# First unit's score granules among the last projections, two sets of part buffers, weight squares one unit later

## The chip, the cores and the metric

The kernel runs on one core of a Trainium2 chip. The metric is the device time of one execution in microseconds; three executions gave 525.33, 525.71 and 528.45, the median is 525.71. The engines work side by side and meet at semaphores only: TensorE (PE, matmuls, with its weight loads as PEld), VectorE (DVE), ScalarE (ACT), GpSimd (POOL), SyncE (SP, which here only issues transfers). Transfers run on 16 DMA engines.

## The reference

One transformer layer on x of 4 batches x 512 tokens x 256 features, float32:

```python
qkv = x @ w_attn + b_attn                      # 16 heads of 16
q, k = rope(q), rope(k)                        # the angle depends on the head
attn = softmax(causal(q @ k.T)) * 256 ** -0.5
x = layernorm(x + (attn @ v) @ w_proj + b_proj)
top 2 of 8 experts by softmax(x @ router_w.T), weights normalised
y = sum over the chosen e: w[e] * (silu(x @ gate_e.T) * (x @ up_e.T)) @ w2_e.T    # FF = 512
x = layernorm(x + y)
```

## The kernel before, in words

**Projections (lines 268 to 422).** TensorE projects each batch in float32: for the four column blocks c of queries and keys two matmuls of 512 columns into bank c (`L416`), then the values of four token tiles (`L397`) into banks 4 to 6 in turn. The rotation is folded into the weights beforehand. Each query and key block is split into three bfloat16 parts whose sum is the float32 value. ScalarE adds the bias (`QF`, L311) and rounds to the first part (`PB[c][:, 0]`, L315); VectorE subtracts to the rest `R1` (L380); ScalarE rounds the rest to the middle part (L303); VectorE subtracts again to the last part (`last_part`, L374). VectorE also adds the values' bias (`values`, L369). The semaphore `l` counts last parts.

There is one buffer `PB[c]` of parts per block for all batches. SyncE stores it to `qk_dram` after the last part (L532, two transfers a block, 8 a batch), and ScalarE may only round the next batch into it when that store has landed (`s_pb`). Between the batches' stores SyncE issues the seven loads (L520, `load_unit`) of one unit of batch 0. All of these are issued in one order on one queue: stores of batch b, loads of unit (0,b), next b; then `XB`, then the eight 1 MB loads of the expert weights w1 (L526), then the loads of unit (1,0) and so on. The loads of unit (b,g) wait until the transposed scores of unit (b-1,g) are done, since they reuse its buffer `KQ[g]`.

**Units (lines 425 on).** A unit is four heads of one batch: 16 units (b,k), each worked on in a step of ten granules n. Within a step the engines carry three units at once. TensorE computes the scores of unit u (`S`, L1168, 96 rows: six products of parts) granule by granule into banks 0 and 1; VectorE reduces each granule to row maxima (L877) and signals `Sf`, on which granule n + 2 waits. GpSimd splits the maxima (L581), TensorE transposes them, ScalarE writes them as extra rows (L747). For unit u - 2 TensorE forms transposed scores into banks 2 to 5 (`ST`, L1189 and L1190), ScalarE takes exponentials (L724), TensorE multiplies with the values (L1207). The order of everything within a step is written out by hand in tables of (k, n). In steps (0,0) and (0,1) ScalarE has no exponentials yet.

The expert weights are scaled by their mean square. `SQUARES_AT` gives the places (b, k, n) at which ScalarE squares the next 4 KB-per-partition piece of w1, 16 pieces in all (L755); a pair needs one landed w1 load. Their sum is formed on TensorE before step (2,0) (L1346).

TensorE starts the units only when all `qf` and all eight value sums are there. GpSimd does nothing in the projections. After the units, 39 expert tiles of 128 tokens follow, and a last normalisation.

Of the kernel before, what the change touches and what calls it, by code (L numbers as in the profile page):

```python
# [24 lines left out]
BF16 = mybir.dt.bfloat16  # L25
# [3 lines left out]
ALU = mybir.AluOpType  # L29
ACT = mybir.ActivationFunctionType  # L30
AX = mybir.AxisListType

P = 128
B, T, E = 4, 512, 256
H, HD = 16, 16
# [3 lines left out]
KC = E // P  # L39
NG = 4  # L40
GH = H // NG
# [27 lines left out]
NSG, NTG = 10, 5  # L69
# [13 lines left out]
def block_kernel(nc, x, xT, w_attn, b_attn, w_proj, b_proj, router_wT, w1T, w2T, cos_sin, cf, cb, kones, tokid, unused, out):  # L83
    ctx = ExitStack()
    with ctx:
# [3 lines left out]
        def sem(name):  # L89
            return ctx.enter_context(nc.semaphore(name))  # L90
# [11 lines left out]
        W1 = sb("W1", [P, SPARE + NUNIT * UNIT])  # L102
# [11 lines left out]
        VR = sb("VR", [P, NTT, E])  # L114
# [64 lines left out]
        WA = W1[:, 0:2304].rearrange("p (k f) -> p k f", k=3)  # L179
# [3 lines left out]
        XTB = [W1[:, 5120 + 1024 * n:6144 + 1024 * n].rearrange("p (k t) -> p k t", k=KC) for n in range(B)]  # L183
        QF = [W1[:, 9216 + 512 * n:9728 + 512 * n] for n in range(4)]
        R1 = [W1[:, 11264 + 512 * n:11776 + 512 * n] for n in range(4)]
        PB = [W1[:, 13312 + 768 * n:14080 + 768 * n].bitcast(BF16).rearrange("p (r t) -> p r t", r=3) for n in range(4)]
        BC = sb("BC", [P, 4])
        ONE = sb("ONE", [P, 1])
        EX0 = sb("EX0", [P, 1])
# [39 lines left out]
        s_const, s_rope, s_x = sem("s_const"), sem("s_rope"), [sem(f"s_x{b}") for b in range(B)]  # L229
        s_sync = {n: sem("a_" + n) for n in ("init", "one", "dve", "wr", "bias", "bc", "ps", "vps", "qf", "h", "r", "m", "l", "v", "rb")}  # L230
        a = s_sync
        s_pb = [sem(f"s_pb{c}") for c in range(4)]

        names = ("S", "Sf", "np", "pool", "qm", "ST", "exp", "pv", "va", "ocp", "ot", "rc", "nrm",
                 "mt", "at", "atc", "ap", "res", "x1", "xb", "tp", "xt", "lgp", "lg", "mc", "rkp", "rk", "mrun", "dve", "dl", "ex",
# [17 lines left out]


        V_AFTER = ((0, 1), (2, 3), (4, 5), (6, 7))

        def rope_views(k):

# [29 lines left out]
        @block.scalar  # L288
        def _(act):
            act.wait_ge(s_wqk[KC - 1], 16)  # L290
            act.dma_start(CF[:, :], cf).then_inc(s_const, 16)
            act.dma_start(CB[:, :], cb).then_inc(s_const, 16)
            for g in range(NG):
                act.dma_start(K[g][SK:SKM, :, :], kones[0:MPARTS * GH]).then_inc(s_const, 16)
            act.dma_start(WP[:, :, :], w_proj.rearrange("c p f -> p c f")).then_inc(s_const, 16)
            act.dma_start(RW[:, :, :], router_wT.rearrange("(k p) e -> p k e", p=P)).then_inc(s_const, 16)
            act.dma_start(BP[:, :], b_proj.partition_broadcast(P)).then_inc(s_const, 16)
            act.dma_start(TOK[:, :], tokid).then_inc(s_const, 16)
            act.dma_start(DUMP[:, :], unused).then_inc(s_const, 16)

            def middle_part(b, c):
                act.wait_ge(a["r"], 4 * b + c + 1)
                act.activation(PB[c][:, 1, :], R1[c], ACT.Copy).then_inc(a["m"], 1)  # L303

            act.wait_ge(a["bc"], 1)
            for b in range(B):
                for c in range(4):
                    act.wait_ge(a["ps"], 4 * b + c + 1)
                    if b:
                        act.wait_ge(a["l"], 4 * (b - 1) + c + 1)  # L310
                    act.activation(QF[c], bank[c], ACT.Identity, bias=BC[:, c:c + 1]).then_inc(a["qf"], 1)  # L311
                    act.wait_ge(a["qf"], 4 * b + c + 1)
                    if b:
                        act.wait_ge(s_pb[c], 32 * b)
                    act.activation(PB[c][:, 0, :], QF[c], ACT.Copy).then_inc(a["h"], 1)  # L315
                    if c:
                        middle_part(b, c - 1)
                middle_part(b, 3)

        @block.vector  # L320
        def _(dve):
            t = Tally()
# [40 lines left out]
            dve.wait_ge(a["bias"], 1)  # L363
            dve.tensor_copy(BC[:, :], MISC[:, 0:4]).then_inc(a["bc"], 1)

            def values(v):

                dve.wait_ge(a["vps"], v + 1)
                dve.tensor_tensor(VR[:, 2 * v:2 * v + 2, :], bank[4 + v % 3].rearrange("p (n f) -> p n f", n=2),  # L369
                                  WA[:, 2, 2 * E:3 * E].unsqueeze(1).broadcast_to([P, 2, E]), ALU.add).then_inc(a["v"], 1)  # L370

            def last_part(b, c):
                dve.wait_ge(a["m"], 4 * b + c + 1)
                dve.tensor_tensor(PB[c][:, 2, :], R1[c], PB[c][:, 1, :], ALU.subtract).then_inc(a["l"], 1)  # L374

            dve.wait_ge(s_bv, 16)
            for b in range(B):
                for c in range(4):
                    dve.wait_ge(a["h"], 4 * b + c + 1)
                    dve.tensor_tensor(R1[c], QF[c], PB[c][:, 0, :], ALU.subtract).then_inc(a["r"], 1)  # L380
                    if c:
                        last_part(b, c - 1)
                last_part(b, 3)
                for v in V_AFTER[b]:
                    values(v)

        @block.tensor
        def _(pe):
            def values(v):

                pe.wait_ge(s_x[v // 2], 16)
                if v >= 3:
                    pe.wait_ge(a["v"], v - 2)
                for n in range(2):
                    t0 = (2 * (v % 2) + n) * P
                    for k in range(KC):
                        last = nc.tensor.matmul(bank[4 + v % 3][:, n * E:(n + 1) * E], XTB[v // 2][:, k, t0:t0 + P],  # L397
                                                WA[:, k, 2 * E:3 * E], start=(k == 0), stop=(k == KC - 1))
                last.then_inc(a["vps"], 1)

            def biases():

                pe.wait_ge(a["rb"], 1)
                pe.wait_ge(a["one"], 1)
                for c in range(4):
                    last = nc.tensor.matmul(MISC[:, c:c + 1], WR[0:1, 2, c * P:(c + 1) * P], ONE[0:1, :], start=True, stop=True)
                last.then_inc(a["bias"], 1)

            pe.wait_ge(a["wr"], KC)
            for b in range(B):  # L410
                pe.wait_ge(s_x[b], 16)
                for c in range(4):
                    if b:
                        pe.wait_ge(a["qf"], 4 * (b - 1) + c + 1)
                    for k in range(KC):
                        last = nc.tensor.matmul(bank[c], WR[:, k, c * P:(c + 1) * P], XTB[b][:, k, :], start=(k == 0), stop=(k == KC - 1))  # L416
                    last.then_inc(a["ps"], 1)
                if b == 0:
                    biases()
                    pe.wait_ge(s_wv, 16)  # L420
                for v in V_AFTER[b]:
                    values(v)


        def after(first, *waits):
# [12 lines left out]
        def early(b, k, n):  # L438
# [20 lines left out]

        SQUARES_AT = {(0, 1, 9): (0, 2), (0, 2, 1): (2, 3), (0, 2, 5): (3, 4), (0, 3, 1): (4, 6), (0, 3, 9): (6, 7), (1, 0, 1): (7, 9),
                      (1, 0, 9): (9, 10), (1, 1, 1): (10, 11), (1, 1, 9): (11, 12), (1, 2, 1): (12, 13), (1, 2, 9): (13, 14),
                      (1, 3, 1): (14, 15), (1, 3, 5): (15, 16)}
        X1_HIGH_AT, STORE_AT, ROWS_AT = (3, 9), (0, 5), (1, 6)


# [22 lines left out]
        def live(b, k, lag):  # L490

            if not isinstance(b, int):
                return True
            return 0 <= b * NG + k - lag < NU
# [17 lines left out]
        def _(sp):  # L512
# [10 lines left out]
            def load_w1(n):  # L523

                at = n * 4 * UNIT
                sp.dma_start(W1[:, SPARE + at:SPARE + at + 4 * UNIT], w1T[:, at:at + 4 * UNIT]).then_inc(s_w1[n], 16)  # L526

            for b in range(B):
                for c in range(4):
                    sp.wait_ge(a["l"], 4 * b + c + 1)  # L530
                    for n in range(2):
                        sp.dma_start(qk_dram[c // 2, b, (c % 2) * 2 + n, :, :, :, :].rearrange("r d h t -> (d h) r t"),  # L532
                                     PB[c][n * GH * HD:(n + 1) * GH * HD, :, :]).then_inc(s_pb[c], 16)
                if b == 0:
                    for c in range(4):
                        sp.wait_ge(s_pb[c], 32)
                load_unit(0, b)
            for c in range(4):
                sp.wait_ge(s_pb[c], 32 * B)
            sp.dma_start(XB[:, :, :], x[0:T, :].rearrange("(n p) f -> p n f", p=P)).then_inc(s_xb, 16)  # L540
            sp.wait_ge(a["v"], 8)
            for n in range(NUNIT // 4):
                load_w1(n)

            def load_w2(n):
                sp.dma_start(W2[n], w2T[:, n * NX * E:(n + 1) * NX * E]).then_inc(s_w, 16)
# [11 lines left out]
        def _(pool):  # L558
# [58 lines left out]
            def weights_low(u):  # L617
# [3 lines left out]
                                   ALU.subtract).then_inc(s["lop"], 1)  # L621
                pool.wait_ge(s["lop"], on_pool(u))

            pool.wait_ge(s_const, 11 * 16)
            pool.wait_ge(a["v"], 8)
            def step(b, k, tails=True, routing=True):
# [234 lines left out]
        def _(dve):  # L861
# [233 lines left out]
            dve.tensor_scalar(ACC[:, 0:P], ONESF[:, :], DF[:, :], None, ALU.mult)  # L1095
            link(dve.tensor_scalar(ACC[:, P:NCOL], ONESF[:, 0:NTILES], DF[:, :], None, ALU.mult))
            dve.wait_ge(s_zero, 2 * 16)
            for k in range(NG):
                step(0, k, False, False)
            for k in range(NG):  # L1100
                step(1, k, routing=False)
# [53 lines left out]
        def _(pe):  # L1155
# [129 lines left out]
            def step(b, k, tails=True, routing=True):  # L1285
# [9 lines left out]
                for n in range(NSG):  # L1295
# [14 lines left out]
                    if n == OT_AT and live(b, k, 3):  # L1310
                        outputs_T(b, k, reader)
                        reader = (s["nrm"], u - 2)
                    if n == MAXT_AT and live(b, k, 1):
                        maxT(b, k)
                    if tails and (k, n) in AT_AT:
                        h = AT_AT[k, n]
# [15 lines left out]
                        mm(bank[0][:, 0:NX], onesb, MRUN[:, :], start=True, stop=True).then_inc(s["cnt"], 1)  # L1332

            pe.wait_ge(s_const, 11 * 16)
            pe.wait_ge(a["qf"], 4 * B)
            pe.wait_ge(a["v"], 8)
            for k in range(NG):
                step(0, k, False, False)
            for k in range(NG):
                step(1, k, routing=False)  # L1340
# [214 lines left out]
```

## Time and profile before

| what | value |
|---|---|
| median of three executions | 525.71 us |
| the profiled execution | 523.54 us, its span 521.4 us |
| mean granted TensorE clock | 0.936 |
| busy: TensorE, VectorE, ScalarE, GpSimd | 441.9, 309.5, 273.4, 226.7 us |
| moved by DMA | 57.23 MB, mean 110 GB/s |

The difference between execution and span is what lies around the first and last instruction. Busy shares are averages over stages with different limits: projections to about 55 us, units to about 285 us, experts to about 495 us, then the last normalisation. The change touches the first two.

### The profile page before, as it was taken

The numbers are of one execution on the slowest core, as the hardware profiler recorded it, in microseconds if no ns is written. First come the engines' busy times: TensorE is split into PE (matmuls) and PEld (weight loads), VectorE is DVE, ScalarE is ACT, GpSimd is POOL, SyncE is SP. The second block draws the span as 40 slices with busy tenths as digits, with TensorE's granted clock in tenths as the row PEclk, the third lists the DMA queues.
The fourth block names the chain that finished last, engine by engine and source line by source line (L and its number), as shares of the span: only waits on it lengthen the run. The fifth ranks groups of instructions, "written<-read, shape, count | busy, mean of one in ns | idle before, by whom it ended". The sixth has DMA issues, their size and how long they took to land.

```text
span 521.4 us, 9268 instructions
## 1 busy us (share of the span) xinstructions
PE 441.9 (85%) x2920; PEld 269.4 (52%) x2920; DVE 309.5 (59%) x1108; ACT 273.4 (52%) x386; POOL 226.7 (43%) x314
## 2 busy tenths in 40 slices
PE   2999589899987899889936899999999999999900
PEld 0555224445553555445513567666667666666600
DVE  6275998877779887987697334465323332232224
ACT  0476349998867668665938334532333323323215
POOL 0000021112675567655844376554555655655322
PEclk9999759999999999989977799999999999999965
DMA  8378899222146324422320114343323333233164
GB/s 278 59 207 246 259 379 369 76 64 78 55 131 203 122 62 111 134 61 83 127 76 11 30 31 92 51 89 54 57 49 61 52 53 62 44 58 52 21 158 185
DMA packets 32976, 57.23 MB, mean 110 GB/s; under 512 B 5025, under 2 KB 23585, under 8 KB 31394
## 3 DMA queue, kind: packets, MB, share of 16 engines
q1 hardware_dynamic: 18306, 39.60, 23.8%
q0 software_dynamic: 7488, 10.27, 12.3%
q10 hardware_dynamic: 7136, 6.77, 4.3%
q8 instruction: 26, 0.43, 0.4%
q14 instruction: 20, 0.16, 0.1%
HBM read 38.64 MB, written 17.97 MB: 109 GB/s over the span
## 4 chain that ended last, share of the span: by engine, by line
PE 58%; DVE 23%; ACT 9%; DMA 4%; issue 4%; SPq 1%; ACTq 0%; DVEq 0%; POOLq 0%
PE PS L1371 20%; PE PS L1398 12%; DVE PS L877 8%; PE PS L1207 5%; PE PS L1168 4%; PE PS L1390 3%; PE PS L1242 3%; PE PS L1189 2%; DVE B L981 2%; ACT PT L724 2%; PE PS L416 2%; PE PS L1363 2%; DMA qk_parts<-W 2%; PE PS L1261 1%; DMA sum_rows<-PT,IDXA 1%
## 5 line engine op out<-in xcount | busy, mean ns | idle before, releaser
L877 DVE CUSTOM_DVE_ANT_0 PS<-PS,CB 128x512 f32<-128x512 f32 (+3 forms) x256 | 120.4, 514 | 29.8 <-PE PS L1168 28.7
L1371 PE MATMUL PS<-W,PT 128*128 x468 | 114.9, 382 | 1.9 <-ACT PT L826 1.6
L724 ACT ACTIVATE PT<-PS 128x1024 f32<-128x1024 f32 x80 | 81.3, 1022 | 36.3 <-PE PS L1190 35.7
L683 POOL DMA_INDIRECT sum_rows<-PT,IDXA x39 | 62.0, 1591 | 70.3 <-ACT PT L837 65.1
L1168 PE MATMUL PS<-KQ 96*128 96x512 bf16 (+3 forms) x256 | 66.9, 327 | 19.7 <-DVE MX L877 14.1
L1126 DVE SCALAR_TENSOR_TENSOR PT<-PS,CW,PT 128x512 f32<-128x512 f32 x39 | 29.3, 750 | 68.1 <-ACT PT L830 68.1
L1371 PEld LDWEIGHTS PS<-W,PT 128*128 128x128 f16 x468 | 44.4, 98 | 41.0 <-issue 4.0
L1189 PE MATMUL PS<-KQ 104*128 104x512 bf16 (+3 forms) x256 | 61.0, 310 | 1.1 <-ACT PT L724 1.1
L1132 DVE COPY PT<-PS 128x512 f32<-128x512 f32 x39 | 27.0, 691 | 52.3 <-PE PS L1390 52.3
L826 ACT ACTIVATE PT<-PS 128x512 f16<-128x512 f16 x39 | 23.3, 597 | 63.2 <-PE PS L1363 63.2
L837 ACT ACTIVATE PT<-PS,WS 128x256 f32<-128x256 f32 x39 | 18.5, 474 | 72.0 <-PE PS L1398 72.0
L581 POOL TENSOR_SCALAR NM<-MX 128x16 f32<-128x16 f32 x16 | 4.3, 268 | 118.8 <-DVE MX L877 118.6
L676 POOL DMA_INDIRECT KQ<-x_rows,IDXA x39 | 40.1, 1029 | 21.2 <-POOL IDXA L666 7.7
L1207 PE MATMUL PS<-PT,VA 128*32 128x256 f32 (+3 forms) x512 | 46.1, 456 | 2.8 <-ACT KQ L747 1.8
L1190 PE MATMUL PS<-CB 128*128 128x128 bf16 x256 | 48.4, 224 | 0.0
L1168 PEld LDWEIGHTS PS<-KQ 96*128 96x128 bf16 x256 | 19.5, 100 | 54.8 <-DVE MX L877 37.9
L1398 PE MATMUL PS<-KQ,PT 128*128 x156 | 40.1, 380 | 0.9 <-DVE PT L1132 0.9
L1398 PE MATMUL PS<-W,PT 128*128 x156 | 40.0, 379 | 0.0
L416 PE MATMUL PS<-W 128*128 128x512 f32 x64 | 30.5, 633 | 10.2 <-DVE W L351 10.2
L747 ACT ACTIVATE KQ<-PS 8x2048 bf16<-8x2048 bf16 x16 | 29.9, 1870 | 16.6 <-PE PS L1217 16.4
L877 DVE DVE_READ_ACCUMULATOR2_ANT MX<- 128x1 f32 x256 | 36.3, 142 | 0.0
L1189 PEld LDWEIGHTS PS<-KQ 104*128 104x128 bf16 x256 | 25.8, 101 | 17.2 <-ACT PT L724 4.2
(183 smaller groups left out, 740.9 us busy)
## 6 DMA issues: line engine op xcount, KB each, us to landing
W<-w1T SPq DMA_DIRECT2D x8, 1024.0 KB, 14.5
qk_parts<-W SPq DMA_DIRECT2D x32, 192.0 KB, 3.1
KQ<-qk_parts SPq DMA_DIRECT2D x32, 192.0 KB, 2.9
KQ<-qk_parts SPq DMA_DIRECT2D x64, 64.0 KB, 2.8
x_rows<-X1S ACTq DMA_DIRECT2D x4, 516.0 KB, 3.5
W<-xT SPq DMA_DIRECT2D x4, 512.0 KB, 6.8
KQ<-qk_parts SPq DMA_DIRECT2D x16, 128.0 KB, 2.9
sum_rows<-X ACTq DMA_DIRECT2D x4, 512.0 KB, 3.1
```

What stands on the lines that cost most here:

```text
L416: last = nc.tensor.matmul(bank[c], WR[:, k, c * P:(c + 1) * P], XTB[b][:, k, :], start=(k == 0), stop=(k == KC - 1))
L676: pool.indirect_dma_start(XGR[q], None, rows, bass.IndirectOffsetOnAxis(ap=IDXA[:, j, 0:1], axis=0)).then_inc(s_g[q], 16)
L683: pool.indirect_dma_start(acc_dram, bass.IndirectOffsetOnAxis(ap=IDXA[:, j, 0:1], axis=0), YS[j % TRIO], None, compute_op=ALU.add).then_in ...
L724: act.activation(PT[n][:, :], STb[slot_of(k, n)].rearrange("p a n -> p (a n)"), ACT.Exp).then_inc(s["exp"], 1)
L747: act.activation(Q[g][SK:SKM, :, :], maxb[SK:SKM, 0:T].unsqueeze(1).broadcast_to([MPARTS * GH, GH, T]), ACT.Copy).then_inc(s["qm"], 1)
L877: last = dve.tensor_tensor_reduce(src, src, maskS[:, TT * P - w:], 1.0, LOW, ALU.add, ALU.max, MX[p][:, h, i:i + 1])
L1168: last = mm(dst[:, at:at + w], Q[p][0:SK, h, i * P:(i + 1) * P], K[p][0:SK, h, 0:w], start=True, stop=True)
L1189: mm(dst[:, at:at + T - j * P], K[g][0:SKM, h, j * P:(j + 1) * P], Q[g][0:SKM, h, j * P:T], start=True, stop=False)
L1190: last = mm(dst[:, at:at + P], identb, maskT, start=False, stop=True)
L1207: last = mm(Ob[32 * h:32 * h + 32, j * P:T], VA[p][:, j, h, :], PT[gr][:, bk * T + at:bk * T + at + T - j * P], start=(j == 0), stop=(j == ...
L1371: last = mm(dst, XGT[j % TRIO][:, x_part, k, :], w1h[:, bass.ds(at, UNIT)], start=(k == x_part == w_part == 0), stop=(k == KC - 1 and x_pa ...
L1398: last = mm(YP[:, 0:E], HT[:, k, :], W2[k][:, bass.ds(e * E, E)], start=(k == 0), stop=(k == FF // P - 1))
```

## The change

- Parts get two sets of buffers, `PB[b % 2][c]`; the second set lies in the space of `W2[2]` and `W2[3]`. Semaphores `s_pb` are doubled with them. ScalarE waits for a store only from batch 2 on, for that of two batches before. SyncE waits for the second set's last stores after it has issued the w1 loads.
- The last part of every block is computed on GpSimd, all 16 before its first unit.
- The last batch's projections are issued among the ten granules of step (0,0): key and query block c after granule c + 1, into bank c + 2; the halves of the two value projections after granules 5 to 8, into banks 7 and 6. VectorE's subtraction for block c follows its reduction of granule c + 2, and the two value sums follow granules 7 and 9. TensorE waits for all `qf` and value sums at the maxima's transpose of step (0,1) instead of before step (0,0).
- The weight squares begin at (0,2,9) instead of (0,1,9) and still end at (1,3,5).

```diff
-        PB = [W1[:, 13312 + 768 * n:14080 + 768 * n].bitcast(BF16).rearrange("p (r t) -> p r t", r=3) for n in range(4)]
+        PB = [[v.bitcast(BF16).rearrange("p (r t) -> p r t", r=3) for v in half] for half in (
+            [W1[:, 13312 + 768 * n:14080 + 768 * n] for n in range(4)],
+            [W2[2 + n // 2][:, n % 2 * 768:n % 2 * 768 + 768] for n in range(4)])]
...
+        V_BANK = (4, 5, 6, 4, 5, 6, 7, 6)
...
-                    act.activation(QF[c], bank[c], ACT.Identity, bias=BC[:, c:c + 1]).then_inc(a["qf"], 1)
+                    act.activation(QF[c], bank[c + 2 * (b == B - 1)], ACT.Identity, bias=BC[:, c:c + 1]).then_inc(a["qf"], 1)
                     act.wait_ge(a["qf"], 4 * b + c + 1)
-                    if b:
-                        act.wait_ge(s_pb[c], 32 * b)
-                    act.activation(PB[c][:, 0, :], QF[c], ACT.Copy).then_inc(a["h"], 1)
+                    if b >= 2:
+                        act.wait_ge(s_pb[c][b % 2], 32)
+                    act.activation(PB[b % 2][c][:, 0, :], QF[c], ACT.Copy).then_inc(a["h"], 1)
...
-        SQUARES_AT = {(0, 1, 9): (0, 2), (0, 2, 1): (2, 3), (0, 2, 5): (3, 4), (0, 3, 1): (4, 6), (0, 3, 9): (6, 7), (1, 0, 1): (7, 9),
-                      (1, 0, 9): (9, 10), (1, 1, 1): (10, 11), (1, 1, 9): (11, 12), (1, 2, 1): (12, 13), (1, 2, 9): (13, 14),
-                      (1, 3, 1): (14, 15), (1, 3, 5): (15, 16)}
+        SQUARES_AT = {(0, 2, 9): (0, 2), (0, 3, 1): (2, 3), (0, 3, 5): (3, 4), (0, 3, 9): (4, 6), (1, 0, 1): (6, 7), (1, 0, 9): (7, 9),
+                      (1, 1, 1): (9, 10), (1, 1, 9): (10, 11), (1, 2, 1): (11, 12), (1, 2, 9): (12, 13), (1, 3, 1): (13, 14),
+                      (1, 3, 5): (14, 16)}
...
             for c in range(4):
-                sp.wait_ge(s_pb[c], 32 * B)
+                sp.wait_ge(s_pb[c][0], 64)
             sp.dma_start(XB[:, :, :], x[0:T, :].rearrange("(n p) f -> p n f", p=P)).then_inc(s_xb, 16)
             sp.wait_ge(a["v"], 8)
             for n in range(NUNIT // 4):
                 load_w1(n)
+            for c in range(4):
+                sp.wait_ge(s_pb[c][1], 64)
...
+            for b in range(B):
+                for c in range(4):
+                    pool.wait_ge(a["m"], 4 * b + c + 1)
+                    pool.tensor_tensor(PB[b % 2][c][:, 2, :], R1[c], PB[b % 2][c][:, 1, :], ALU.subtract).then_inc(a["l"], 1)
...
-            for k in range(NG):
+            for n in range(NSG):
+                reduces(0, 0, n)
+                if 2 <= n < 6:
+                    rounded_rest(dve, B - 1, n - 2)
+                elif n in (7, 9):
+                    values_out(dve, 6 + (n - 7) // 2)
+            for k in range(1, NG):
                 step(0, k, False, False)
...
+                        if (b, k) == (0, 1):
+                            pe.wait_ge(a["qf"], 4 * B)
+                            pe.wait_ge(a["v"], 2 * B)
                         maxT(b, k)
...
-            pe.wait_ge(a["qf"], 4 * B)
-            pe.wait_ge(a["v"], 8)
-            for k in range(NG):
+            pe.wait_ge(s_x[B - 1], 16)
+            for n in range(NSG):
+                if n < 2:
+                    pe.wait_ge(a["qf"], 4 * (B - 2) + n + 1)
+                S(0, 0, n)
+                if 1 <= n < 5:
+                    c = n - 1
+                    if c < 2:
+                        pe.wait_ge(a["qf"], 4 * (B - 2) + c + 3)
+                    else:
+                        pe.wait_ge(a["v"], c + 2)
+                    project(bank[c + 2], B - 1, c)
+                elif 5 <= n < 9:
+                    v = 6 + (n - 5) // 2
+                    pe.wait_ge(a["bc"], 1)
+                    pe.wait_ge(a["v"], 6)
+                    project_values(v, (n - 5) % 2)
+            for k in range(1, NG):
                 step(0, k, False, False)
```

`project`, `project_values`, `rounded_rest` and `values_out` are the old loops' bodies as functions; `project_values` takes its bank from `V_BANK`.

## Rows read from the trace of the kernel before

**Rows 1.** Timeline of TensorE, 40 to 60: start us, us, engine, line, operation, tiles, count, [idle before].

```profile
44.75 7.03 PE L416 MATMUL PS<-W 128*128 128x512 f32 x16
51.61 3.62 PE L397 MATMUL PS<-W 128*128 128x256 f32 x16
59.29 1.01 PE L1168 MATMUL PS<-KQ 96*128 96x512 bf16 x2 [4.06 <-DVE VR L369]
```

**Rows 2.** Timeline of VectorE, 57 to 68.

```profile
57.75 1.28 DVE L369 TENSOR_TENSOR VR<-PS,W 128x512 f32<-128x512 f32 x2
...
59.82 0.24 DVE L1096 TENSOR_SCALAR ACC<-ONESF,DF 128x39 f32<-128x39 f32 x1
60.09 0.70 DVE L877 CUSTOM_DVE_ANT_0 PS<-PS,CB 128x512 f32<-128x512 f32 x1
...
67.80 0.70 DVE L877 CUSTOM_DVE_ANT_0 PS<-PS,CB 128x512 f32<-128x512 f32 x1
```

**Rows 3.** Timeline of ScalarE, 40 to 109.

```profile
40.11 0.63 ACT L315 ACTIVATE W<-W 128x512 bf16<-128x512 f32 x1 [3.08 <-DMA qk_parts<-W]
...
76.89 1.02 ACT L724 ACTIVATE PT<-PS 128x1024 f32<-128x1024 f32 x1 [1.53 <-PE PS L1190]
...
86.79 1.02 ACT L724 ACTIVATE PT<-PS 128x1024 f32<-128x1024 f32 x1 [1.12 <-PE PS L1190]
...
97.67 1.02 ACT L724 ACTIVATE PT<-PS 128x1024 f32<-128x1024 f32 x1
...
107.44 1.05 ACT L755 ACTIVATE W<-W 128x1024 f32<-128x1024 f32 x1
...
108.61 1.02 ACT L724 ACTIVATE PT<-PS 128x1024 f32<-128x1024 f32 x1
```

**Rows 4.** Timeline of the SyncE queue, 24 to 71 (duration: all issues of the row).

```profile
24.79 6.06 SPq L532 DMA_DIRECT2D qk_parts<-W  x8
...
36.42 5.40 SPq L532 DMA_DIRECT2D qk_parts<-W  x8
...
65.36 5.77 SPq L526 DMA_DIRECT2D W<-w1T  x8
```

**Rows 5.** Last w1 loads and last loads of unit (1,0): issue, landing.

```profile
L526 SPq DMA_DIRECT2D W<-w1T x3: 451/485/746, 69.4 to 70.6; - x3
...
DMA to landing us min/median/max: 16.0/20.0/23.0
...
L520 SPq DMA_DIRECT2D KQ<-qk_parts x2: 423/426/428, 87.6 to 88.1; - x2
...
DMA to landing us min/median/max: 4.9/6.1/7.4
```

**Rows 6.** Busy time by stretches; last columns: granted clock, DMA share, GB/s.

```profile
87.00:88.00 1.00, 1.00 (x12) 0.35 (x13) 0.86 (x3) 1.00 (x2) 0.29 (x2) 1.00 1.02 385
...
94.00:95.00 1.00, 1.00 (x14) 0.48 (x7) 0.10 (x1) 1.00 (x2) 0.00 (x0) 1.00 0.06 25
```

**Rows 7.** Timeline of TensorE, starts of units (0,2) and (1,0).

```profile
75.20 0.58 PE L1168 MATMUL PS<-KQ 96*128 96x512 bf16 x1 [0.29 <-DVE MX L877]
...
95.38 0.38 PE L1168 MATMUL PS<-KQ 96*128 96x256 bf16 x2
...
96.69 0.39 PE L1168 MATMUL PS<-KQ 96*128 96x512 bf16 x1
```

**Rows 8.** Two lines of GpSimd: duration ns min/median/max, starts, shape.

```profile
L620 POOL TENSOR_TENSOR W<-WLO,W x15: 1151/1154/1163, 151.0 to 277.8; 128x512 f16<-128x512 f32 x15
...
L606 POOL TENSOR_TENSOR XB<-XB,BP x4: 2349/2372/2385, 118.3 to 266.4; 128x1024 f32<-128x1024 f32 x4
```

**Rows 9.** Chain that ended last, 138 to 146: start us, us, what.

```profile
140.38 0.19 ACT W L755
...
142.02 0.66 PE PS L1251 x4
```

**Rows 10.** Busy time by short stretches, TensorE idle from 55.23 on.

```profile
58.00:59.00 1.00, 0.00 (x0) 0.00 (x0) 1.00 (x3) 0.00 (x0) 0.00 (x0) 1.00 0.87 255
59.00:59.50 0.50, 0.21 (x1) 0.14 (x2) 0.47 (x6) 0.00 (x0) 0.00 (x0) 0.72 0.87 258
```

More of the change, by code:

```diff
@@ L231, in block_kernel @@
         a = s_sync
-        s_pb = [sem(f"s_pb{c}") for c in range(4)]
+        s_pb = [[sem(f"s_pb{c}{n}") for n in range(2)] for c in range(4)]
         names = ("S", "Sf", "np", "pool", "qm", "ST", "exp", "pv", "va", "ocp", "ot", "rc", "nrm",
@@ L255, in block_kernel, with rounded_rest, values_out, project @@
         V_AFTER = ((0, 1), (2, 3), (4, 5), (6, 7))
+        V_BANK = (4, 5, 6, 4, 5, 6, 7, 6)
+        def rounded_rest(dve, b, c):
+            dve.wait_ge(a["h"], 4 * b + c + 1)
+            dve.tensor_tensor(R1[c], QF[c], PB[b % 2][c][:, 0, :], ALU.subtract).then_inc(a["r"], 1)
+        def values_out(dve, v):
+            dve.wait_ge(a["vps"], v + 1)
+            dve.tensor_tensor(VR[:, 2 * v:2 * v + 2, :], bank[V_BANK[v]].rearrange("p (n f) -> p n f", n=2),
+                              WA[:, 2, 2 * E:3 * E].unsqueeze(1).broadcast_to([P, 2, E]), ALU.add).then_inc(a["v"], 1)
+        def project(dst, b, c):
+            for k in range(KC):
+                last = nc.tensor.matmul(dst, WR[:, k, c * P:(c + 1) * P], XTB[b][:, k, :], start=(k == 0), stop=(k == KC - 1))
+            last.then_inc(a["ps"], 1)
+        def project_values(v, n):
+            t0 = (2 * (v % 2) + n) * P
+            for k in range(KC):
+                last = nc.tensor.matmul(bank[V_BANK[v]][:, n * E:(n + 1) * E], XTB[v // 2][:, k, t0:t0 + P],
+                                        WA[:, k, 2 * E:3 * E], start=(k == 0), stop=(k == KC - 1))
+            if n:
+                last.then_inc(a["vps"], 1)
         def rope_views(k):
@@ L302, in middle_part @@
                 act.wait_ge(a["r"], 4 * b + c + 1)
-                act.activation(PB[c][:, 1, :], R1[c], ACT.Copy).then_inc(a["m"], 1)
+                act.activation(PB[b % 2][c][:, 1, :], R1[c], ACT.Copy).then_inc(a["m"], 1)
             act.wait_ge(a["bc"], 1)
@@ L364, in _ @@
             dve.tensor_copy(BC[:, :], MISC[:, 0:4]).then_inc(a["bc"], 1)
[L366 to L374, printed above, removed]
             dve.wait_ge(s_bv, 16)
-            for b in range(B):
+            for b in range(B - 1):
                 for c in range(4):
[L379 to L383, printed above, removed]
+                    rounded_rest(dve, b, c)
                 for v in V_AFTER[b]:
-                    values(v)
+                    values_out(dve, v)
         @block.tensor
         def _(pe):
[L389 to L399, printed above, removed]
             def biases():
@@ L409, in _ @@
             pe.wait_ge(a["wr"], KC)
-            for b in range(B):
+            for b in range(B - 1):
                 pe.wait_ge(s_x[b], 16)
@@ L414, in _ @@
                         pe.wait_ge(a["qf"], 4 * (b - 1) + c + 1)
-                    for k in range(KC):
-                        last = nc.tensor.matmul(bank[c], WR[:, k, c * P:(c + 1) * P], XTB[b][:, k, :], start=(k == 0), stop=(k == KC - 1))
-                    last.then_inc(a["ps"], 1)
+                    project(bank[c], b, c)
                 if b == 0:
@@ L421, in _ @@
                 for v in V_AFTER[b]:
-                    values(v)
+                    if v >= 3:
+                        pe.wait_ge(a["v"], v - 2)
+                    for n in range(2):
+                        project_values(v, n)
         def after(first, *waits):
@@ L532, in _ @@
                         sp.dma_start(qk_dram[c // 2, b, (c % 2) * 2 + n, :, :, :, :].rearrange("r d h t -> (d h) r t"),
-                                     PB[c][n * GH * HD:(n + 1) * GH * HD, :, :]).then_inc(s_pb[c], 16)
+                                     PB[b % 2][c][n * GH * HD:(n + 1) * GH * HD, :, :]).then_inc(s_pb[c][b % 2], 16)
                 if b == 0:
                     for c in range(4):
-                        sp.wait_ge(s_pb[c], 32)
+                        sp.wait_ge(s_pb[c][0], 32)
                 load_unit(0, b)
             for c in range(4):
-                sp.wait_ge(s_pb[c], 32 * B)
+                sp.wait_ge(s_pb[c][0], 64)
             sp.dma_start(XB[:, :, :], x[0:T, :].rearrange("(n p) f -> p n f", p=P)).then_inc(s_xb, 16)
```

## The prediction

> **What bounds the kernel now.** I read TensorE's timeline first [rows 1]. The four batches of projections follow one another without a gap. The last one starts at 44.75 us and ends at 51.61 + 3.62 = 55.23, and TensorE then stands idle for 4.06 us until the first score matmul at 59.29. The reader should see two things. The projections are bound by TensorE, and nothing of the scores runs beside them. VectorE's timeline says what fills the gap [rows 2]: the last subtractions, two value sums from 57.75 to 59.03 (0.64 each), small constants to 60.06. Then the first unit's ten score granules take 60.09 to 67.80, which is 7.71 us.
>
> ScalarE's timeline says what bounds the units after that [rows 3]. From the first exponential of the unit (0,3) at 86.79 to that of (1,0) at 97.67 it has nearly no gap. The 10.88 us hold five exponentials, the broadcast of the maxima and three weight squares. The square starts at 107.44 and the next exponential at 108.61, so a square costs 1.17 us there.
>
> The SyncE queue comes third and decides this forecast [rows 4]. Its first store is issued at 24.79, and from 36.42 to 65.36 the issues stand end to end: 8 stores of the parts, 7 loads of a unit, and again, three times. The eight 1 MB loads of w1 start only when that backlog is through. The landings are next [rows 5]. The last w1 load is issued at 70.6 and lands 23.0 us later, at 93.6. The last of the seven loads of unit (1,0), issued at 88.1, lands 7.4 us later, at 95.5. By bandwidth [rows 6] the stream is over long before: 385 GB/s at 87 us, 25 at 94. The tail is a share of 0.06 of 16 engines, one DMA engine that lags. The first score matmul of (1,0) starts at 96.69 [rows 7], so this load has 1.2 us to spare today.
>
> **The change part by part. First unit among the last projections.** TensorE's own work of the last batch is 55.23 - 44.75 = 10.5 us. Ten granules come in between. No row shows them at full clock without waits, so I bound one: 0.2 us if it hides in the pipeline and 0.63 at most, as at half clock [rows 1]. I take 0.3, as two of its matmuls at full clock take 0.38 together with an overlap [rows 7], so 3.0 in sum, and TensorE is through at 58.3. VectorE has 7.7 of granules, and four subtractions and two value sums at 0.64, together 11.5 us, and 1.0 of constants first, less than TensorE's 13.5. The chain to a subtraction (bias and rounding on ScalarE, 0.63 each) is shorter than the next projection (7.03 / 4 = 1.76), so no granule waits in lockstep. After TensorE the last granule (0.8) and the last value sum (0.6) remain, with 0.6 for handovers: the second unit starts at 60.3 instead of 67.80, **7.5 us earlier**. With granules at 0.2 or 0.63 it is 8.5 or 4.2.
>
> **Last part on GpSimd, two sets of buffers.** Sixteen subtractions leave VectorE (about 0.64 each). GpSimd's nearest rows are 1.15 for a 128x512 and 2.37 for a 128x1024 one [rows 8], so I take 1.15, with 2.37 as the bad end. In batches 0 to 2 TensorE has no wait on them, so they cost the path nothing. The new buffers take away ScalarE's waits for stores (3.08 us at 40.11 the longest [rows 3]); TensorE ran without a gap past those, so that is worth nothing either, and only lets VectorE reach the first granule at 46.6. But SyncE's first store waits for GpSimd: about 0.4 us later than 24.79. Everything behind it on SyncE is a backlog and shifts with it: w1's first load from 65.36 to 65.8. The value sums it also waits for are done at 60. Unit (0,0)'s loads land at 40, before 44.9: free.
>
> So the compute side moves 7.5 us earlier and **the w1 stream does not move**. The first unit's score transposes, which release (1,0)'s loads, finish at 77 instead of 84, so those loads are issued while all DMA engines are full of w1 and stand behind it on the engine that lags. I let them land 0.4 later than now, at 95.9.
>
> **Squares one unit on.** Two squares that stood at (0,1,9), where ScalarE had no exponential to do, now come where it is full. At (0,2,9) two in a row hold the next unit's first exponential 0.6 us (its scores now come at 86.79; the fifth exponential before it would end about 85.1 without squares among them, and two squares make 87.4); unit (0,3) has four instead of three (+1.17); unit (1,3) has three instead of two (+1.17). In (1,3) the chain before runs exponential, square, exponential, x1 columns, TensorE's transposes, the sum of squares [rows 9], so the square lies on the path. Their price lies between 0 (idle elsewhere takes it) and 2 x 1.17 + 0.6 = 2.9.
>
> **The sum.** TensorE would reach unit (1,0)'s first matmul at 96.69 - 7.5 + 0.6 = 89.8. The load lands at 95.9, so it stands idle 6 us, and 6.7 of the 7.5 us are given back; the squares at (0,2) to (0,3) hide under the same wait. What is left at (1,0) is 96.69 - 95.9 = 0.8 us of gain. The granted clock adds to it: it fell to half (1.2 GHz) 4.0 us into the idle stretch of [rows 1, 10], and at half clock first score matmul to exponential took 75.20 to 76.89 = 1.69 us, against 96.69 to 97.67 = 0.98 at full clock [rows 3, 7]. I charge 0.7 (0 if the clock stays). Then 1.17 in (1,3). Profiled execution: 523.54 - 0.8 + 0.7 + 1.2 = 524.6. The median of the runs lies 2.2 us above that execution (525.71), so **526.8 us**.
>
> **A rule against the change.** The rows of GpSimd's 128x512 operation spread only from 1.151 to 1.163 us [rows 8] beside a VectorE that was mostly busy, so I put no contention into the sum. The Trainium skill, "SBUF — State Buffer", section "Who interferes with whom", says that a VectorE instruction with two SBUF inputs and a GpSimd instruction that reads SBUF exclude each other for the whole instruction. By it each of batch 0's four subtractions could wait for a VectorE one (0.64): SyncE's chain up to 2.4 us later, and the sum 529.2 instead of 526.8.
>
> **Rivals.** **A, the load is not late.** The lag of one DMA engine may be this execution's. If unit (1,0)'s loads land by 90, what is left is 7.5 - 0.6 - 1.17 - 1.17 = 4.5: 519.0, as a median 521.2. For it: the other engines are done at about 88 to 90 [rows 6]; against: the lag is there in both landings of [rows 5]. Landings between give what lies between. The Trainium skill, "DMA: Bandwidth & Descriptors", section "Queues, rings and completion order", has each DMA engine take descriptors in ring order; by that sentence loads issued earlier behind w1 win nothing, and the trace agrees, with 95.5.
>
> **B, slower.** GpSimd's subtraction takes the 2.37 us of the long row at 128x512. Then batch 0's last part is ready 4.7 us later, SyncE's whole backlog, w1 and (1,0)'s loads move with it, TensorE waits until 100.2, and the run is 526.8 + 4.3 = 531.1. Each 0.1 us above 1.15 costs 0.35, since the four stand in a chain, and slower by over 1% begins at 2.35 us per subtraction. Against it: the narrow spread in [rows 8].
>
> **C, no overlap.** The granules and projections wait for each other and the second unit starts where it does now. Then the load is in time, but all squares count: 525.71 + 2.9 = 528.6. Against it: two granules of slack between score bank and reduction.
>
> **How the numbers follow.** The forecast has 0.58, A with its in-between values 0.22, B 0.08, C 0.07, and 0.05 is for something unseen. About 1% (5.3 us) is what a measurement of this kernel tells from no change. Faster by over 1% needs a median below 520.5: A at its best end (granules at 0.2, a hidden square), 0.11. Slower by over 1% is above 531.0: B and part of the unseen, 0.09. Within: 0.80. The range goes from 521.0, just below A, to 529.5, which holds the forecast with a landing 2.7 us later and C; A's best end and B are out.
>
> **What would show it.** In the changed profile: VectorE's first granule near 46.6 to 47 and the second unit's first near 60.3; GpSimd with sixteen rows of about 1.15 us; w1's first issue within a microsecond of 65.4; TensorE idle about 6 us before the first score matmul of (1,0), released by a DMA, near 95.9, and half clock just after; ScalarE with three squares in (1,3). The forecast is wrong if that matmul starts near 90 (A), if w1's first issue has gone beyond 68 (B), or if the second unit still starts after 66 (C).

## The result and the profile after

The changed kernel takes 528.45 us (median of 22 executions, 526.05 to 533.1) against 526.14 (22 executions) of the kernel before. The ratio is 1.0047 with a 95% interval of 1.0028 to 1.0066, so it is slower by about 2.5 us, or half a per cent. The forecast was 526.8 against a median of 525.71, a loss of 1.1. Its profiled execution took 527.44 us with a span of 525.4, against 523.54 and 521.4.

The overlap came. TensorE's timeline, 44 to 61 us (beside [rows 1]):

```profile
44.37 0.60 PE L1185 MATMUL PS<-KQ 96*128 96x512 bf16 x2
44.80 1.88 PE L275 MATMUL PS<-W 128*128 128x512 f32 x4
47.24 0.39 PE L1185 MATMUL PS<-KQ 96*128 96x512 bf16 x1 [0.55 <-DVE MX L888]
47.46 1.88 PE L275 MATMUL PS<-W 128*128 128x512 f32 x4
...
56.75 1.03 PE L282 MATMUL PS<-W 128*128 128x256 f32 x4
57.62 0.39 PE L1185 MATMUL PS<-KQ 96*128 96x256 bf16 x2
```

L275 is the projection and L1185 the score matmul. The only wait inside the mixed stretch is 0.55 us, before granule 2. VectorE's timeline (beside [rows 2]), first granule of the first unit, last value sum, first granule of the second:

```profile
46.42 0.70 DVE L888 CUSTOM_DVE_ANT_0 PS<-PS,CB 128x512 f32<-128x512 f32 x1
...
58.88 0.69 DVE L269 TENSOR_TENSOR VR<-PS,W 128x512 f32<-128x512 f32 x1
59.48 0.69 DVE L888 CUSTOM_DVE_ANT_0 PS<-PS,CB 128x512 f32<-128x512 f32 x1
```

The second unit starts at 59.48 instead of 67.80, which is 8.3 us of lead; 0.4 of it stood already when the second batch of projections began (23.73 against 24.11), before anything that was changed on TensorE. Now the SyncE queue (beside [rows 4]):

```profile
24.85 6.09 SPq L537 DMA_DIRECT2D qk_parts<-W  x8
33.34 4.17 SPq L525 DMA_DIRECT2D KQ<-qk_parts  x7
37.56 5.47 SPq L537 DMA_DIRECT2D qk_parts<-W  x8
...
66.22 4.08 SPq L531 DMA_DIRECT2D W<-w1T  x8
76.05 58.00 SPq L525 DMA_DIRECT2D KQ<-qk_parts  x35
```

The w1 loads are issued from 66.22 on, 0.9 us later than before. The loads of unit (1,0) are issued from 76.05 on, 8.3 us earlier than the 84.34 of the kernel before, while w1 is under way. The issues and landings of the last two w1 loads and of the last three loads of (1,0) (beside [rows 5]):

```profile
L531 SPq DMA_DIRECT2D W<-w1T x2: 432/496/559, 69.3 to 69.7; - x2
...
DMA to landing us min/median/max: 19.3/21.3/23.4
...
L525 SPq DMA_DIRECT2D KQ<-qk_parts x3: 420/421/422, 78.7 to 79.7; - x3
...
DMA to landing us min/median/max: 13.8/13.9/16.6
```

The reader is to see that 8 us of earlier issue bought nothing: the last w1 load lands at 93.1 (69.7 + 23.4), and the last load of (1,0), issued at 79.7, lands 16.6 us later, at 96.3, against 95.5 before. TensorE and ScalarE at the start of (1,0) (beside [rows 3, 7]):

```profile
87.53 1.07 PE L1224 MATMUL PS<-PT,VA 128*32 128x384 f32 x16 [0.61 <-ACT PT L735]
96.33 0.61 PE L1185 MATMUL PS<-KQ 96*128 96x512 bf16 x1 [7.73 <-DMA KQ<-qk_parts]
```

```profile
98.04 1.02 ACT L735 ACTIVATE PT<-PS 128x1024 f32<-128x1024 f32 x1 [7.44 <-PE PS L1207]
...
107.91 1.02 ACT L735 ACTIVATE PT<-PS 128x1024 f32<-128x1024 f32 x1 [1.20 <-PE PS L1207]
...
111.12 1.00 ACT L735 ACTIVATE PT<-PS 128x1024 f32<-128x1024 f32 x1
```

TensorE stands idle for 7.73 us and starts (1,0) at 96.33 instead of 96.69. From there to the unit after it, the first exponentials are 13.08 us apart (98.04 to 111.12), against 10.94 before. The stretches show why; the last three numbers of a row are the granted clock as a share of 2.4 GHz, the busy share of the 16 DMA engines and their GB/s (beside [rows 6, 10]):

```profile
90.00:92.00 2.00, 0.00 (x0) 0.00 (x0) 0.00 (x0) 0.60 (x2) 0.00 (x0) 1.00 1.03 209
92.00:94.00 2.00, 0.00 (x0) 0.00 (x0) 0.00 (x0) 0.00 (x0) 0.00 (x0) 0.62 1.06 248
94.00:96.00 2.00, 0.00 (x0) 0.00 (x0) 0.00 (x0) 0.00 (x0) 0.00 (x0) 0.50 0.71 152
96.00:98.00 2.00, 1.67 (x6) 0.74 (x6) 0.76 (x2) 0.00 (x0) 0.00 (x0) 0.50 0.06 25
...
100.00:102.00 2.00, 2.00 (x9) 1.25 (x7) 1.24 (x3) 2.00 (x4) 0.37 (x3) 0.50 0.03 8
102.00:104.00 2.00, 2.00 (x18) 1.12 (x16) 1.07 (x7) 1.23 (x2) 0.00 (x0) 0.82 0.00 0
```

The clock fell to 1.2 GHz while TensorE waited and stayed there until about 102.7, some 6.4 us into the work of (1,0).

The same rows show something that the prediction did not have. It read the tail as one DMA engine that lags, and a share of 0.06 is that again, from 96 on. But from 90 to 94 the share is above 1 while only 209 to 248 GB/s move: all 16 engines are busy, at about half the rate of the w1 stream. In that stretch the seven loads of (1,1) are under way too: they were issued from 86.7 to 89.4 and landed 7.2 to 8.6 us later. No run separates what they add to the landing of (1,0)'s loads from what w1's tail does.

### The profile page after: what moved, and what is told of

Its sections match the earlier page's. It is cut to its first block, busy times and chain, and to the rows that moved or that the text cites. A ratio compares the mean times of both kernels' runs of the same rounds, so it can differ in the third digit from the quotient of the medians.

```text
span 525.4 us, 9264 instructions
## 1 busy us (share of the span) xinstructions
PE 441.7 (84%) x2920; PEld 270.6 (51%) x2920; DVE 298.5 (57%) x1092; ACT 273.6 (52%) x386; POOL 245.1 (47%) x330
## 4 chain that ended last, share of the span: by engine, by line
PE 64%; DVE 21%; DMA 6%; ACT 4%; issue 3%; SPq 1%; ACTq 0%; DVEq 0%; POOLq 0%
PE PS L1406 19%; PE PS L1433 12%; DVE PS L888 7%; PE PS L275 5%; PE PS L1185 5%; PE PS L1224 5%; PE PS L1425 3%; DMA KQ<-qk_parts 3%; PE PS L1259 3%; PE PS L1206 3%; PE PS L282 2%; DVE B L992 2%; PE PS L1398 2%; DMA sum_rows<-PT,IDXA 1%; PE PS L1278 1%
## 5 line engine op out<-in xcount | busy, mean ns | idle before, releaser
L1185 PE MATMUL PS<-KQ 96*128 96x512 bf16 (+3 forms) x256 | 65.6, 321 | 22.8 <-DVE MX L888 13.9
L1206 PE MATMUL PS<-KQ 104*128 104x512 bf16 (+3 forms) x256 | 63.8, 320 | 0.2 <-ACT PT L735 0.2
L1207 PE MATMUL PS<-CB 128*128 128x128 bf16 x256 | 49.5, 228 | 0.0
L1185 PEld LDWEIGHTS PS<-KQ 96*128 96x128 bf16 x256 | 20.0, 100 | 57.0 <-DVE MX L888 36.6
L275 PE MATMUL PS<-W 128*128 128x512 f32 x64 | 30.5, 624 | 10.4 <-DVE W L381 10.4
L634 POOL TENSOR_TENSOR W<-W 128x512 bf16<-128x512 f32 x16 | 18.3, 1157 | 38.8 <-ACT W L333 38.8
```

The lines of the kernel that those rows point to most:

```text
L275: last = nc.tensor.matmul(dst, WR[:, k, c * P:(c + 1) * P], XTB[b][:, k, :], start=(k == 0), stop=(k == KC - 1))
L1185: last = mm(dst[:, at:at + w], Q[p][0:SK, h, i * P:(i + 1) * P], K[p][0:SK, h, 0:w], start=True, stop=True)
L1206: mm(dst[:, at:at + T - j * P], K[g][0:SKM, h, j * P:(j + 1) * P], Q[g][0:SKM, h, j * P:T], start=True, stop=False)
L1207: last = mm(dst[:, at:at + P], identb, maskT, start=False, stop=True)
```

## The experiments

Each was timed against the kernel before on the same chip; an "us" behind a ratio is the ratio times 526.14. The yardstick inside the traces, one profiled execution each, is the time of the first exponential of a unit, because what follows unit (2,0) varies from execution to execution (last section). "(1,0)" means the step in which TensorE scores unit (1,0); the exponentials in it belong to the unit two before. The times vary a little from the start, whatever the kernel: the second batch of projections begins between 23.29 us (e7) and 24.80 (e9), at 24.11 in the kernel before.

| kernel | ratio, interval | (1,0) | (1,1) | (2,0) |
|---|---|---|---|---|
| before | 1 | 97.67 | 108.61 | 145.76 |
| changed | 1.0047, 1.0028 to 1.0066 | 98.04 | 111.12 | 149.42 |
| e1_old_squares | 0.9986, 0.9964 to 1.0008 | 97.03 | 107.97 | 145.11 |
| e2_load_between | 0.9855, 0.9821 to 0.9889 | 91.23 | 102.08 | 140.38 |
| e3_keep_busy | 1.0034, 1.0008 to 1.006 | 97.84 | 108.72 | 147.02 |
| e4_squares_alone | 1.0015, 0.999 to 1.004 | 98.69 | 109.54 | 147.85 |
| e5_gpsimd_alone | 1.002, 0.9999 to 1.0042 | 97.94 | 108.87 | 146.01 |
| e6_load_between_before | 1.0007, 0.9988 to 1.0026 | 98.09 | 109.03 | 146.17 |
| e7_spread_squares | 0.9861, 0.9817 to 0.9904 | 89.02 | 102.44 | 140.96 |
| e8_changed_again | 1.0069, 1.0041 to 1.0098 | 100.00 | 112.43 | 150.73 |
| e9_two_loads_between | 0.9815, 0.9781 to 0.9849 | 89.61 | 99.38 | 136.53 |
| e10_order_no_overlap | 0.9941, 0.9915 to 0.9966 | 99.56 | 109.33 | 146.47 |

**The wait for the loads.** e2 changes SyncE's order alone:

```diff
-            for n in range(NUNIT // 4):
+            for n in range(4):
                 load_w1(n)
             for c in range(4):
                 sp.wait_ge(s_pb[c][1], 64)
+            load_unit(1, 0)
+            for n in range(4, NUNIT // 4):
+                load_w1(n)
...
-                for g in range(NG):
+                for g in range(b == 1, NG):
```

> The changed kernel with SyncE's order changed: four w1 loads, then the seven loads of unit (1,0), then the other four w1 loads. Theory W: the loads of (1,0) land near 81 instead of 96.3, TensorE does not wait at (1,0) and its clock does not fall there; first exponential of (1,0) near 90.7 instead of 98.0 (7.4 us), the unit after it 2.1 us shorter: 528.4 - 9.5 = about 519, 0.986 of the kernel before. Rival G: the wait at (1,0) hides something else that is as late; no faster than 525.

Measured: 0.9855, which is 518.5 us, and in the trace the loads of (1,0) land 4.6 to 6.5 us after issue:

```profile
L525 SPq DMA_DIRECT2D KQ<-qk_parts x7: 331/422/1169, 76.8 to 80.2; - x7
...
DMA to landing us min/median/max: 4.6/4.9/6.5
```

(1,0) starts its exponentials at 91.23 instead of 98.04, and (1,1) follows 10.85 us later. Seven transfers moved ahead of four w1 loads turn a loss of 0.5% into a gain of 1.4%. (Since they wait for the transposed scores of the first unit, the second half of w1 is issued late as well, from 80.67 on.) The control has the same order on the kernel before:

> The kernel before with only SyncE's order changed: four w1 loads, loads of unit (1,0), four w1 loads. Theory W: before the change the loads of (1,0) land 1.2 us ahead of their use, so an earlier landing buys nothing, 1.000 (within 1 us of 526). If the w1 stream bounds the kernel before as well, in a way the trace does not show: 2 us faster or more, below 0.996.

Measured: 1.0007. The loads' place buys nothing here without the lead of the compute side, and the lead nothing without the loads' place: the two are worth something together.

**Is the late landing of single executions only?** The changed kernel as it is, measured again beside the later experiments:

> The changed kernel unchanged, beside the others on one chip, for the landings' spread: the last of the seven loads of (1,0) should again land 15 to 18 us after its issue and TensorE wait 7 to 8 us before (1,0), released by a DMA, with half clock after it. If the lag of one DMA engine were of single executions only, this wait would be 1 to 3 us here. Ratio 1.005.

Measured: 1.0069; the wait was even longer, and the last landing came 18.1 us after issue. In e3 below, with the same order of loads, it came 17.4 us after issue. So the late landing stands in all three traces that have this order and this lead.

```profile
98.29 0.61 PE L1185 MATMUL PS<-KQ 96*128 96x512 bf16 x1 [9.34 <-DMA KQ<-qk_parts]
```

**The squares.** e1 is the changed kernel with `SQUARES_AT` of the kernel before:

> The changed kernel with the weight squares back at their old places, all else kept. Theory W (the changed kernel gives its 8 us lead back because the loads of unit (1,0) land behind w1, and pays about 2.8 us of half clock after that wait and 1.2 us for the third square in (1,3)): ScalarE now waits for the first w1 load at (0,1,9), until about 72, which delays unit (0,2) by about 6 us; but that delay falls into the wait at (1,0), which shrinks from 7.7 to 2 to 3 us, too short for the clock to fall. So the run gains 2.8 + 1.2 = 4 us over the changed kernel: about 524.4, 0.997 of the kernel before. Rival G (the loss sits in the projections or in GpSimd's last parts): nothing is gained, and the 6 us of ScalarE's wait come on top: about 534.

Measured: 0.9986, or 525.4 us, and in the trace 4.3 us less than the changed kernel at (2,0). Rival G falls. The mechanism came out more sharply than I put it: no wait at (1,0) is left at all, since ScalarE itself waits for the first w1 load, and the lead ends there instead.

```profile
73.54 1.06 ACT L766 ACTIVATE W<-W 128x1024 f32<-128x1024 f32 x1 [9.53 <-DMA W<-w1T]
```

So the w1 stream takes the lead either way, and it is cheaper where ScalarE waits. That is not because TensorE is spared idle time: it waits too, 5.27 us until 76.97, and its clock is at 1.2 GHz until after 82. But step (1,0) then runs at full clock. The 4.3 us are 1.0 at (1,0), 2.1 within it (10.94 us instead of 13.08) and 1.2 for the third square in (1,3). e4 is the other half, the new table on the kernel before:

> The kernel before with nothing changed but the weight squares, at their new places. Theory W: no wait for the loads of (1,0) (they land at 95.5 and are wanted near 97.3), so every moved square counts: 0.6 + 1.17 + 1.17 = 2.9 us slower, about 529.0, 1.0055 of the kernel before. Rival F (a square costs nothing where it is put, idle time elsewhere takes it): 526.1, 1.000.

Measured: 1.0015 with an interval of 0.999 to 1.004, between the two. The trace has 2.1 us at (2,0): 1.0 by (1,0), 1.1 in the unit (1,3). By steps: the two squares in (0,2) cost 0.53 us (0.6 expected), the fourth square in (0,3) only 0.49 (1.17 expected), the third in (1,3) 1.18. In (0,3) the kernel before had idle time of ScalarE, 0.29 us before one exponential alone, which the square could fill.

**The clock.** e3 keeps TensorE busy during the wait:

```diff
+            pe.wait_ge(s["nrm"], 1)
+            for n in range(24):
+                mm(MISC[:, 0:T], identb, maskS, start=True, stop=True)
             for k in range(NG):
                 step(1, k, routing=False)
```

> The changed kernel with 24 matmuls of 512 columns (results unused) on TensorE between the units (0,3) and (1,0), about 5.2 us of work inside the 7.7 us wait. Theory W: TensorE is then idle only some 2.5 us before the loads land, the granted clock stays at full, and the half-clock part of the loss goes: 2 to 2.8 us faster than the changed kernel, about 525.8, 0.9995 of the kernel before. Rival H (the clock costs only the 0.7 us of the forecast, the rest is something else in unit (1,0)): 527.7. If the added work itself delays unit (1,0): above 528.5.

In the trace the clock stayed at 2.4 GHz through the wait, which ended with 3.27 us of idle time, and unit (1,0) took 10.88 us from first exponential to first exponential instead of 13.08:

```profile
94.00:96.00 2.00, 0.00 (x0) 0.00 (x0) 0.00 (x0) 0.00 (x0) 0.00 (x0) 1.00 0.99 203
96.00:98.00 2.00, 1.14 (x10) 0.57 (x13) 0.71 (x2) 0.16 (x1) 0.00 (x0) 1.00 0.24 64
```

```profile
96.86 0.39 PE L1185 MATMUL PS<-KQ 96*128 96x512 bf16 x1 [3.27 <-DMA KQ<-qk_parts]
```

From first matmul to exponential (1,0) took 0.98 us again instead of 1.71. So the half clock costs 0.7 + 2.2 = 2.9 us; the loads landed 0.5 us later in this execution (TensorE starts at 96.86 instead of 96.33), which leaves the 2.4 us by which it is ahead of the changed kernel at (2,0). Whole runs say less: 1.0034 against 1.0047, whose intervals overlap, and 1.0034 is 527.9 us, next to rival H's 527.7 and not the theory's 525.8. The clock's price is shown in the unit, not in the run's time.

**GpSimd and the buffers alone**, on the kernel before:

> The kernel before with only the last parts on GpSimd and the two sets of part buffers; projections, granules and squares as before. Theory W: TensorE's four batches have no wait on either, so nothing is gained but the shorter tail on VectorE after the last projection (its three last subtractions, at most 1.3 us earlier first granule), and that runs into the same w1 stream: 0 to 1.3 us faster, 0.9975 to 1.000. Rival G (GpSimd's subtractions block VectorE's or set SyncE's stores back): 1 to 3 us slower, 1.002 to 1.006.

Measured: 1.002 (0.9999 to 1.0042), a little above the theory's range and at the low end of the rival's. The trace shows more lead than I expected: the first granule is reduced at 56.71 instead of 60.09 and the second unit starts at 64.26 instead of 67.80, because ScalarE no longer lags behind stores and VectorE's tail is shorter (0.4 us of it are the earlier start of this execution). Of the lead 1.3 us are left at (0,2), where ScalarE waits for w1:

```profile
73.20 1.06 ACT L756 ACTIVATE W<-W 128x1024 f32<-128x1024 f32 x1 [4.33 <-DMA W<-w1T]
```

The rest goes in (0,3), where the clock stood at 1.2 GHz from about 92.5 to 95.9; (1,0) comes at 97.94, no earlier than before.

**Better versions.** e7 is e2 with the squares spread by ScalarE's idle time:

```diff
-        SQUARES_AT = {(0, 2, 9): (0, 2), (0, 3, 1): (2, 3), (0, 3, 5): (3, 4), (0, 3, 9): (4, 6), (1, 0, 1): (6, 7), (1, 0, 9): (7, 9),
-                      (1, 1, 1): (9, 10), (1, 1, 9): (10, 11), (1, 2, 1): (11, 12), (1, 2, 9): (12, 13), (1, 3, 1): (13, 14),
-                      (1, 3, 5): (14, 16)}
+        SQUARES_AT = {(0, 2, 9): (0, 2), (0, 3, 1): (2, 3), (0, 3, 5): (3, 4), (0, 3, 9): (4, 5), (1, 0, 1): (5, 6), (1, 0, 9): (6, 7),
+                      (1, 1, 1): (7, 8), (1, 1, 9): (8, 9), (1, 2, 1): (9, 10), (1, 2, 7): (10, 12), (1, 2, 9): (12, 13),
+                      (1, 3, 1): (13, 15), (1, 3, 5): (15, 16)}
```

> The changed kernel with the loads of (1,0) between the w1 loads and the squares spread anew: 2, 3, 2, 2, 4, 3 in the units (0,2) to (1,3), two of the four of (1,2) at n = 7, where ScalarE stood idle 2.29 us, two at (1,3,1) and one at (1,3,5). Theory: a square costs 1.17 us only where ScalarE has no idle time; against e2_load_between one such square leaves each of (0,3), (1,0) and (1,3): 3.5 us faster, about 515, 0.979 of the kernel before. Rival F (squares are absorbed wherever they stand, other engines bound the units): as e2_load_between, 0.9855.

Measured: 0.9861, no better than e2. The forecast failed, but not as rival F had it: (1,0) came 2.2 us earlier than in e2 (1.0 of it from the earlier start of this execution, the rest about one square), and then the same kind of wait stood one unit on. The second half of w1 lies ahead of the loads of (1,1), in e2 too, but there TensorE came later and waited 0.17 us.

```profile
101.28 0.39 PE L1188 MATMUL PS<-KQ 96*128 96x512 bf16 x1 [3.40 <-DMA KQ<-qk_parts]
```

After this wait the clock fell to 1.2 GHz until about 105.3, and the unit took 11.14 us from first exponential to first exponential, against 9.75 in e2. In e3 TensorE had stood idle nearly as long, 3.27 us, after 5.35 us of matmuls without a gap, and the clock stayed at 2.4 GHz. So a wait of this length can cost its clock or not.

e9 puts the loads of (1,1) between the last w1 loads as well (four w1, (1,0), two w1, (1,1), two w1):

> The changed kernel with the spread squares of e7_spread_squares and SyncE's order four w1 loads, loads of (1,0), two w1 loads, loads of (1,1), two w1 loads. In e7 TensorE waited 3.4 us for the loads of (1,1), issued behind w1's second half, which took the gain of the spread squares. Theory W: that wait goes too; first exponential of (2,0) near 137 instead of 141.0, the run about 515, 0.979 of the kernel before. Rival F (spread squares gain nothing by themselves): as e2_load_between, 0.9855.

Measured: 0.9815, or 516.4 us, with the first exponential of (2,0) at 136.53 as expected, and no wait for loads in any unit. Its interval (0.9781 to 0.9849) still touches those of e2 and e7; the trace has it 3.9 us ahead of e2 at (2,0). By its median this is the fastest version, 1.9% below the kernel before; that it beats e2 and e7 is shown in the trace, not in whole runs. Without the overlap the same order and squares give e10:

> The kernel before, so without overlap, GpSimd or second buffers, with the same order of loads and the same squares as e9. It shows what the overlap is worth where no load holds it back. Theory W: the second unit starts 7.6 us later than in e9 (67.8 instead of 60.2) and nothing takes that up: 522 to 523, 0.993, 7 to 8 us above e9. Rival: the w1 stream or the squares pace these units whatever the start, and the two lie within 3 us.

Measured: 0.9941, 6.6 us above e9 (by the two intervals, some 4.4 to 8.8), and 9.9 us at (2,0) in the traces. The traces overstate it: e10's second unit starts at 69.77, 2.0 us later than in the kernel before, 0.6 of it from the start and most of the rest from longer waits of ScalarE for stores (4.24 us the longest). With the loads out of the way the overlap, together with GpSimd and the buffers, is worth about the 7.5 us that were forecast, and the rival falls. e10 is also 0.6% faster than the kernel before, clear of noise, without any overlap; no run separates its order of loads from its squares. (e6, with only the loads of (1,0) moved, gained nothing.)

## Why the prediction was right

By its own steps:

- **Overlap of the first unit.** Forecast 7.5 us of lead with the second unit at 60.3, measured 8.3 at 59.48. The total was right, its split was not: the prediction gave all of it to the overlap and called the buffers "worth nothing", but in e5 the buffers and GpSimd alone bring the second unit to 64.26, 3.5 us earlier, and the overlap adds 4.8. TensorE's granules cost close to the 0.2 end of the bound; VectorE's first granule came at 46.42 (46.6 forecast).
- **GpSimd's last part.** Sixteen rows of 1.149 to 1.169 us, as taken (1.15). The first store came 0.06 us later, not 0.4; w1's first issue 0.9 later, not 0.4, mostly because one group of seven loads took 4.17 us to issue instead of 3.11. Rival B had no ground. What the Trainium skill says on exclusion ("SBUF — State Buffer", "Who interferes with whom") stays open: the two kinds of subtraction took turns here and hardly met. The one of VectorE that began 0.2 us before the end of one of GpSimd, at 29.23, took 0.76 us instead of 0.69. (Four times 0.64 is 2.6, not the 2.4 us of the prediction; nothing hangs on it.)
- **The w1 stream does not move.** This was the step on which all hung, and it held: landing of (1,0)'s loads 96.3 (95.9 forecast), TensorE ready at 88.6 (89.8), wait 7.73 (6), start of (1,0) 0.36 us ahead of before (0.8). e2 shows that the place of these loads behind w1 is what makes TensorE wait, e6 that it costs nothing without the lead, e8 that it repeats. Of rival A nothing was seen in three executions. The picture of one lagging engine is incomplete: all 16 were busy up to 94.
- **The clock.** Forecast 0.7, measured more: 1.71 us instead of 0.98 from first matmul to exponential (0.7, as forecast) and then 2.1 us more within the unit. This is the term of the sum that was mis-sized. The half clock lasted 6.4 us into the unit's work, and behind the first exponential TensorE, not ScalarE, set the pace: ScalarE stood idle three times for TensorE (0.45, 0.77 and 1.20 us, the last before 107.91), where it had had 0.29 us before. The prediction charged nothing for this part and gave no reason. The kernel before had shown such a stretch, from 75.20 to about 79.7, and I read only its first 1.7 us. e3 takes the half clock away and puts the term at 2.9 us instead of 0.7.
- **Third square in (1,3).** Forecast 1.17; from the first exponential of (1,3) to that of (2,0) 15.88 us instead of 14.70, so 1.18. e4 has the same 15.88. (The squares in (0,2) and (0,3), 0.6 and 1.17 forecast, hid under the wait as forecast; in e4, where nothing hides them, they cost 0.53 and 0.49.)

At (2,0) these make -0.36 + 0.73 + 2.14 + 1.18 = 3.7 us with roundings, the 149.42 - 145.76 of the traces; the forecast had 1.1, the runs' ratio gives 2.5 (1.5 to 3.5). Single executions differ as much behind (2,0) (last section), so one trace and the runs agree no better than this. The runs settle that the change is a loss; the sizes of its terms come from the traces. Rivals A, B and C did not occur. That the time fell into the range owes something to luck: the upper end, 529.5, had been set for a later landing and for rival C, and the room served for a clock term of 2.9 us that had been put at 0.7.

## What to carry to other kernels

A stage that is pulled forward runs into the next thing that was not: before moving compute, look at which transfer has the least time to spare at its use (here it landed 1.2 us before 96.69), and whether its issue or what lies ahead of it in the queue decides when it lands. If it is what lies ahead, split the large transfer and put the small urgent one between. And when an engine is to wait longer, price what its clock does afterwards over the whole stretch at half clock, not to the first instruction that depends on it.

## What the runs showed of the hardware

- Seven transfers of 0.8 MB in all, issued 8 us earlier behind the same 8 MB, landed no earlier (96.3 and 95.5). In the changed kernel the mean rate fell from 414 GB/s (86 to 88 us) to 209 (90 to 92) while the busy share of the DMA engines stayed at 1.01 to 1.06 up to 94 and the last of these transfers was still 4 to 6 us away. The end of a backlog is read from the landings; the bandwidth shows it too early.
- After a wait of TensorE for 3.27 us (e3) the clock was still at 2.4 GHz, after 3.40 us (e7) it fell as the work began and stayed at 1.2 GHz for some 3.4 us. During the waits of 7.73 and 9.34 us (changed, e8) it fell before their end.
- From the first exponential of (2,0) to the end of the span equal work took 373.9 us (e9), 375.6 (before), 376.0 (changed), 377.5 (e10) and 379.6 (e2). The two executions of the changed kernel differ by 1.5 us there (376.0 and 377.5). Stretches of half clock lie at different places in these traces: behind 140 us they add up to some 40 us in e9, 46 before, 47 in the changed kernel and 58 in e2. Of the 71 executions of the kernel before that ran beside the experiments, the 12 with a mean granted clock of 0.939 or more took 524.2 us on average, the 10 with 0.930 or less 526.9. So part of the spread of 3 to 8 us among executions of one kernel goes with the clock; not all of it (e7, with 49 us of half clock, needs 378.7 us behind (2,0), the changed kernel with 47 only 376.0), and no run shows it as the cause. This is why the table reads the traces at (2,0).
